# Attention and expert FFN on one core: first loads reordered, router product narrowed, last chunk finished in halves

## The reference, cut

```python
x = x + xattn(_layernorm(x), ctx, ctx, mask, Wq, Wk, Wv, Wo, W1, b1, W2, b2, gamma, beta)   # 8 heads of 128
x = x + ffn(_layernorm(x), router_w, bias, gate_w, up_w, down_w, sh_gate_w, sh_up_w, sh_down_w)

# xattn: q, k, v per head; A = softmax(mask(q @ k.T)); proj = (A @ v) @ Wo
x = _layernorm(value + proj, gamma[0], beta[0])
x = _layernorm(x + relu(x @ W1 + b1) @ W2 + b2, gamma[1], beta[1])

# ffn: 16 experts in 4 groups, 2 groups and 4 experts kept per token, 2 shared experts for all
topk_idx, tw = _route(x, router_w, bias)
y = einsum('etf,efd->etd', silu(h) * u, down_w)           # h, u: gate and up products of each expert
routed = einsum('etd,te->td', y, combine)
sh = silu(x @ sh_gate_w) * (x @ sh_up_w) @ sh_down_w
```

## Time and profile before

| | |
|---|---|
| time, median of 3 runs | 303.92 us (303.61 to 304.14) |
| the profiled execution: its own time | 303.7 us |
| its span, first to last instruction | 301.9 us |
| TensorE busy | 288.1 us, 95% |
| VectorE, GpSimd, ScalarE busy | 189.1, 183.4, 157.6 us |
| mean granted TensorE clock | 0.999 |

### The profile page before, as it was taken

The page is one execution under the profiler, slowest core; times in us unless marked ns, Lnnn a source line. Parts: engine busy times, 40 slices in busy tenths (PEclk is TensorE's granted clock), DMA queues, the critical chain, the costliest instruction groups (busy, mean ns, idle before and its releaser), DMA issues.

```text
span 301.9 us, 4524 instructions
## 1 busy us (share of the span) xinstructions
PE 288.1 (95%) x1446; PEld 209.1 (69%) x1446; DVE 189.1 (63%) x490; ACT 157.6 (52%) x292; POOL 183.4 (61%) x165
## 2 busy tenths in 40 slices
PE   2799999999999999999999999999999999999974
PEld 2566667857774788787677766776678888678853
DVE  0456787558758785764568544366956665866673
ACT  1457727768586468643435253372256455545551
POOL 2336678555377684105878856566507778988870
PEclk9999999999999999999999999999999999999999
DMA  6993600030001100007431342310055345343001
GB/s 220 261 281 67 253 0 3 0 106 1 2 0 34 73 0 1 2 0 275 154 113 53 116 134 85 127 72 0 2 150 210 139 108 182 126 141 112 29 2 69
DMA packets 8711, 27.97 MB, mean 93 GB/s; under 512 B 1136, under 2 KB 1904, under 8 KB 8560
## 3 DMA queue, kind: packets, MB, share of 16 engines
q1 hardware_dynamic: 8400, 26.63, 27.3%
q10 hardware_dynamic: 288, 1.05, 0.9%
HBM read 26.49 MB, written 1.18 MB: 92 GB/s over the span
## 4 chain that ended last, share of the span: by engine, by line
PE 95%; DVE 2%; DMA 2%; ACT 1%; issue 0%; DVEq 0%
PE bank L1394 17%; PE bank L1396 16%; PE bank L1395 16%; PE bank L1605 10%; PE bank L1480 10%; PE bank L1468 6%; PE bank L1440 5%; PE bank L1449 3%; PE bank L1511 2%; PE bank L1504 2%; PE bank L1545 2%; DMA w_in<-in_w_attn 2%; DVE act_lo L1191 1%; PE bank L1533 1%; PE bank L1611 1%; PE bank L1413 1%
## 5 line engine op out<-in xcount | busy, mean ns | idle before, releaser
L474 POOL TENSOR_TENSOR k_T<-xnT,k_T 128x512 f32<-128x512 f32 x64 | 94.3, 1479 | 40.4 <-DVE xnT L1186 25.1
L747 ACT ACTIVATE xnT<-bank 128x512 f32<-128x512 f32 x72 | 43.0, 599 | 76.3 <-PE bank L1396 76.2
L1186 DVE TENSOR_TENSOR xnT<-bank,xnT 128x512 f32<-128x512 f32 x64 | 43.9, 690 | 54.4 <-PE bank L1396 26.9
L1394 PE MATMUL bank<-mT_hi,we_hi 128*128 128x512 f32 x144 | 60.4, 420 | 0.0
L1396 PE MATMUL bank<-mT_hi,we_lo 128*128 128x512 f32 x144 | 56.8, 395 | 0.0
L1395 PE MATMUL bank<-mT_lo,we_hi 128*128 128x512 f32 x144 | 56.8, 394 | 0.0
L1480 PEld LDWEIGHTS bank<-vo,o_T 128*128 128x128 f32 x256 | 30.0, 192 | 5.5 <-issue 3.8
L1605 PE MATMUL bank<-k_T,w_in 128*128 128x512 f32 x72 | 33.0, 592 | 0.0
L1394 PEld LDWEIGHTS bank<-mT_hi,we_hi 128*128 128x128 f32 x144 | 27.1, 188 | 8.2 <-issue 2.3
L1395 PEld LDWEIGHTS bank<-mT_lo,we_hi 128*128 128x128 f32 x144 | 27.1, 188 | 7.2 <-issue 1.7
L1480 PE MATMUL bank<-vo,o_T 128*128 128x128 f32 x256 | 32.1, 279 | 0.0
(11 more groups left out here) (126 smaller groups left out, 492.0 us busy)
## 6 DMA issues: line engine op xcount, KB each, us to landing
k_T<-comb_dram SPq DMA_DIRECT2D x32, 512.0 KB, 3.7
w_in<-in_w_gu SPq DMA_DIRECT2D x3, 768.0 KB, 4.2
w_in<-in_w_dn SPq DMA_DIRECT2D x1, 1152.0 KB, 7.2
w_in<-in_w_attn ACTq DMA_DIRECT2D x2, 512.0 KB, 5.4
w_in<-in_w_attn SPq DMA_DIRECT2D x2, 512.0 KB, 10.7
out_x<-ctx_all SPq DMA_DIRECT2D x4, 256.0 KB, 3.3
ctx_swap<-in_ctx_in SPq DMA_DIRECT2D x2, 384.0 KB, 14.3
ctx_all<-in_ctx_in SPq DMA_DIRECT2D x2, 256.0 KB, 6.4
```

Source lines behind the costliest of these rows:

```text
L474: pool.tensor_tensor(act[n % 4], s_u[n % 2], comb[u % RING][:, c % 2 * CW:(c % 2 + 1) * CW], ALU.mult).then_inc(weighed_ready, 1)
L747: a.activation(silu[n % 2], h_bank[n % 2][:], ACT.Silu).then_inc(silu_ready, 1)
L1186: v.tensor_tensor(into, u_bank[n % 2][:], silu[n % 2], ALU.mult).then_inc(s_u_ready, 1)
L1394: pe.matmul(dst, w_hi, m_hi, start=start, stop=False)
```

## The change

- **Loads.** ScalarE's queue now carries the first chunk of the context, the first chunk of x, and Wq and Wk in four quarters of two heads. SyncE's queue begins with the mask column and then waits until the second quarter has landed before it issues anything else.
- **Start on TensorE.** `turn_ctx(0)` comes first, then folds of two heads each; the first two keys stand behind three of the four quarters. Both folds of Wv and Wo stand ahead of `scores(0)`.
- **Router.** `route` multiplies with the 16 router columns alone.
- **Last chunk.** Steps 69, 70 and 71 are f32 products again. Chunk 3 is copied out, turned (into two free banks), added and stored in two halves. `act_low` stands two steps back.
- **Order.** Most of the lists between the start and step 41 are written in a new order. Normalisation 2 of chunks 2 and 3 is on ScalarE. `gate(0)` and `gate(1)` stand ahead of `router_sigmoid(0)`, and `dn_low` 1 to 3 stand some 20 steps earlier.

```diff
-        ld_w = [[sem(f"ld_w{i}{half}") for half in range(2)] for i in range(2)]
+        ld_w = [[sem(f"ld_w0{q}") for q in range(HP)], [sem(f"ld_w1{half}") for half in range(2)]]
-        fold_bank = [bank[6], bank[5], bank[2], bank[3]]
+        fold_bank = [bank[6], bank[5], bank[2], bank[3], bank[2], bank[3]]
+        SPLIT_TO = N - 3
+        def split(n):
+            return SPLIT_FROM <= n < SPLIT_TO
         def split_count(n):
+        last_bank = [h_bank[0], u_bank[0]]
...
-            context(0, 1, ld_c0)
             sp.dma_start(mask_col[:], mask_tok).then_inc(ld_mask_col, 16)
-            rows(0, 1, ld_x0)
+            sp.wait_ge(ld_w[0][1], 16)
             context(1, 2, ld_c1)
...
-            sp.wait_ge(fold_done, 4)
+            sp.wait_ge(fold_done, 6)
...
-            def store(c):
-                sp.wait_ge(out_ready, c + 1)
-                sp.dma_start(out[:, c * TPC:(c + 1) * TPC, :], x2[:, c * TPC:(c + 1) * TPC, :]).then_inc(stored, 16)
+            def store(c, half=None):
+                first, count = (0, TPC) if half is None else (half * 2, 2)
+                tiles = slice(c * TPC + first, c * TPC + first + count)
+                sp.wait_ge(out_ready, c + 1 + (half or 0))
+                sp.dma_start(out[:, tiles, :], x2[:, tiles, :]).then_inc(stored, 16)
...
-            store(3)
-            sp.wait_ge(stored, 16 * CH)
+            for half in range(2):
+                store(CH - 1, half)
+            sp.wait_ge(stored, 16 * (CH + 1))
```

On ScalarE and VectorE:

```diff
-            for half in range(2):
-                a.dma_start(w_in[:, 0, half], w_attn[:, 0, half]).then_inc(ld_w[0][half], 16)
+            def quarter(q):
+                pair = slice(q % 2 * 2, q % 2 * 2 + 2)
+                a.dma_start(w_in[:, 0, q // 2, pair], w_attn[:, 0, q // 2, pair]).then_inc(ld_w[0][q], 16)
+            a.dma_start(ctx_all[:, 0:TPC, :], ctx_in[:, 0:TPC, :]).then_inc(ld_c0, 16)
+            a.dma_start(x_all[:, 0:TPC, :], x[:, 0:TPC, :]).then_inc(ld_x0, 16)
+            for q in range(HP):
+                quarter(q)
...
-            def copy_out(c):
+            def copy_out(c, cols=slice(0, CW)):
...
-                a.copy(acc_out[c], acc[c][:]).then_inc(acc_copied[c], 1)
+                a.copy(acc_out[c][:, cols], acc[c][:, cols]).then_inc(acc_copied[c], 1)
...
-                if n - 3 >= SPLIT_FROM:
-                    act_low(n - 3)
+                if n >= 2 and split(n - 2):
+                    act_low(n - 2)
...
-            for n in range(N - 3, N):
-                act_low(n)
             add_out(2)
-            add_out(3)
+            add_out(3, 0)
+            add_out(3, 1)
```

On TensorE, with the new `fold` and `turn_out`:

```diff
-                    last = pe.matmul(xm_bank[c][:, t * P:(t + 1) * P], xm_T[:, t * P:(t + 1) * P], small_T[:],
+                    last = pe.matmul(xm_bank[c][:, t * P:t * P + NE], xm_T[:, t * P:(t + 1) * P], small_T[:, 0:NE],
                                      start=True, stop=True)
...
+            def fold(i, part):
+                pe.wait_ge(ld_w[i][part], 16)
+                if i == 0:
+                    half, heads, a, b = part // 2, range(part % 2 * 2, part % 2 * 2 + 2), 1, 0
+                    into = fold_bank[part]
+                else:
+                    pe.wait_ge(fold_lo, HP - 1 + part)
+                    half, heads, a, b = part, range(HP), 0, 1
+                    into = fold_bank[HP + part]
+                for k, h in enumerate(heads):
+                    last = pe.matmul(into[:, k * P:(k + 1) * P], w_in[:, i, half, h, a, :], w_in[:, i, half, h, b, :],
+                                     start=True, stop=True)
                 last.then_inc(fold_done, 1)
...
-                if n >= SPLIT_FROM:
+                if split(n):
...
+            def turn_out(c, half=None):
+                into = acc[c] if half is None else last_bank[half]
+                first, count = (0, TPC) if half is None else (half * 2, 2)
+                pe.wait_ge(acc_copied[c], 1 if half is None else half + 1)
+                for t in range(first, first + count):
+                    last = pe.transpose(into[:, t * P:(t + 1) * P], acc_out[c][:, t * P:(t + 1) * P], ident[:])
                 last.then_inc(out_turned, 1)
```

More of the change, by code:

```diff
@@ L973, in _ @@
             gate(33)
-            for n in range(34, N):
+            gate(34)
+            gate(35)
+            gate(36)
+            gate(37)
+            act_high(36)
+            copy_out(0)
+            act_high(37)
+            copy_out(1)
+            gate(38)
+            gate(39)
+            act_high(38)
+            gate(40)
+            act_high(39)
+            gate(41)
+            for n in range(42, N):
                 gate(n)
-                if n - 2 >= SPLIT_FROM:
+                if n >= 2 and split(n - 2):
                     act_high(n - 2)
@@ L1640, in _ @@
             key(1, 5)
-            fold(1, 1)
+            turn_probs(0)
             key(1, 6)
-            turn_probs(0)
+            key(1, 7)
+            attend(0)
+            scores(3)
             turn_xn(1)
-            key(1, 7)
-            scores(3)
-            attend(0)
+            turn_ctx(2)
+            project(0)
             turn_probs(1)
-            turn_ctx(2)
             scores(4)
-            project(0)
-            scores(5)
             key(2, 0)
@@ L1673, in _ @@
+            key(2, 6)
+            attend(3)
             turn_probs(4)
+            project(2)
+            turn_probs(5)
+            attend(4)
+            key(2, 7)
             project(3)
-            attend(4)
-            turn_probs(5)
-            key(2, 5)
-            key(2, 6)
+            scores(8)
+            turn_probs(6)
+            attend(5)
+            turn_ctx(3)
             turn_xn(3)
-            key(2, 7)
-            turn_ctx(3)
-            attend(5)
-            scores(8)
@@ L1685, in _ @@
-            key(3, 1)
-            key(3, 0)
-            turn_x1(0)
-            project(4)
-            ffn_up(0, 0)
-            scores(9)
-            turn_probs(6)
+            scores(9)
+            project(4)
+            scores(10)
+            turn_x1(0)
+            turn_probs(7)
+            key(3, 0)
+            scores(11)
+            ffn_up(0, 0)
+            key(3, 2)
+            key(3, 1)
             ffn_up(0, 1)
-            scores(10)
-            turn_probs(7)
+            attend(6)
@@ L1713, in _ @@
-            key(3, 6)
+            attend(9)
+            project(8)
+            turn_probs(10)
             turn_xm(0)
-            project(8)
-            scores(12)
-            turn_probs(10)
+            scores(13)
+            attend(10)
+            turn_probs(11)
             route(0)
-            scores(13)
+            scores(14)
+            project(9)
             turn_x1(1)
-            attend(9)
+            scores(15)
             ffn_up(1, 0)
-            scores(14)
+            project(10)
@@ L1778, in _ @@
             up(12)
+            down(6)
+            down(7)
+            down(8)
+            down(9)
+            turn_xm(2)
             up(13)
[L1780 to L1782 removed]
+            up(14)
             down(10)
[L1784 to L1786 removed]
             down(11)
             down(12)
[L1789 removed]
+            up(15)
             up(16)
             up(17)
+            down(13)
+            down(14)
             up(18)
             up(19)
[L1794 to L1795 removed]
+            up(20)
+            route(2)
             down(15)
```

633 lines of the change are left out of this document (316 added, 317 removed).

## The result

The changed kernel takes **300.24 us** (median of 4 executions, 299.78 to 300.31), the kernel before 303.85 beside it (303.61 to 304.14). The measured ratio is 0.9863, with a 95% interval of 0.9834 to 0.9892; the two medians printed here make 0.988, which lies inside it. So the kernel is 1.2 to 1.4% faster, clearly more than the 0.2% that could be told. The forecast was 299.2 in a range of 296.8 to 301.4. The time lies in the range and 1.0 us above the forecast. The profiled span fell from 301.9 to 298.5 us, 3.4 us, where the terms of the sum made 4.5.

What follows compares the result with a forecast made beforehand. TensorE, busy 95% of the span, was taken as the bound, with gains left at the two ends. 303.7 - 2.7 (start) + 0 (router) + 0.4 (middle) - 2.2 (end) = 299.2 us, range 296.8 to 301.4.

Steps and rivals of the forecast that it cites:

- Start: From launch to the transposes behind the eighth key: 15.6 instead of 18.32, -2.7 us, bounds -1.0 and -3.7.
- the landing: First context load, alone on its queue: estimated 2.5 us from issue, landing at 3.3; upper bound 4.3, landing at 5.1.
- start gives back: Rival at the start: clock or context late, more keys at half pace, only 1.0 us gained, 300.9 us; chance 0.16.
- Its 0.5 us: At the start: if the clock counts from the first fold, 1.0 us later, the rise costs 0.5 us, giving 299.7.
- Router: Routing products, four times 8 instructions: 16 columns instead of 128 save 0, as weight loads are not narrowed; other bound 3.1.
- The rival of 3.1 us: Routing products: moving columns set the pace, 3.1 us less, 296.1 us; half of it, 297.6; chance 0.13.
- Middle: New order between the two ends: waits added and removed sum to +0.4 us, bounds -0.9 and +2.
- `turn_xm(1)` to `route(1)`: Neighbouring steps on TensorE in the middle: copy, last transpose's way and hand-over between them cost +0.8 us.
- `project(14)` to `project(15)`: Neighbouring projections in the middle sharing one bank: `add_ctx` and hand-over between them cost +0.5 us.
- the one on the routing: VectorE's way from logits to weights, 13.95 us, taken as just hidden behind 14.3 us of TensorE work; bound 1 us.
- End: From `down(67)`'s last matmul to the span's end: f32 last steps and halves, 299.7 instead of 301.9, -2.2 us.
- Slower than before: Rival from step 42 on: each `act_low` starts inside a weighing, +0.35 us in 30 steps, 309.7 us; chance 0.05.

Runs made afterwards that it cites:

- the warmed-up kernel: The changed kernel with eighteen 128x128 f32 transposes of the identity matrix ahead of `turn_ctx(0)`: 299.19 us, ratio 0.9836.
- the one with the pairs apart: The changed kernel with `project(14)` between `turn_xm(1)` and `route(1)`, and `route(1)` between the last two projections: 299.34 us, ratio 0.9836.
- two more kernels: The changed kernel with pairs apart, `dn_low(1)` moved and transpose warm-up together, 297.58 us; the same with SyncE waiting for the first weight quarter, 297.73 us.

## Why the prediction was right, and where it was off

- **Start, -2.7 forecast, -2.12 in the trace of after.** The step that failed is the landing, and the clock made up for a part. The context was put at 2.5 us from issue to landing, alone on its queue, an estimate from no row; it took 3.6, with x and the quarters issued behind it from 1.22 on, and `mask_context` began at 4.48. That the quarters would be there when their folds came up, at 5.4, 6.3 and 7.2, is shown by no row or run: they landed at 6.54, 7.22 and 7.87. The first was read at 6.58, 0.25 behind the start of the last transpose. They were just in time because the context was late too; in the warmed-up kernel the folds do wait for them, a little. The first key came at 9.16 instead of 8.15. But by then the clock had all but risen (9.5, as forecast), so that only one key matmul ran slow instead of 1.4 us of them. That 9.5 is luck: the forecast had the rise 5 us behind a first transpose at 4.4, and it came 3.9 us behind one at 5.66. The rise is not at a fixed time: with the same instructions the twelve folds took 2.93 us in after, 2.77 in the kernel with `dn_low(1)` moved and 2.53 in the one with the pairs apart, and the transposes behind the eighth key stood at 16.20, 15.97 and 15.62. The start is thus worth 2.1 to 2.7 us, the upper end being the forecast by another way. How much of it is the quarters and how much the transposes' place, no run separates.
- **The rival "start gives back"** named the right weakness, clock and landing, but the reason given for it fell: transposes raise the clock. Its 0.5 us is what was measured, by way of the landing.
- **Router, 0 forecast.** The eight take 0.91 us in after, 0.89 in the earlier trace rows. The rival of 3.1 us is excluded. For its half, the interval of the kernel with the router alone would leave 0.2 to 1.6 us; its median is 0.2 lower, and the trace, with the same stride and a span 0.1 longer, leaves nothing.
- **Middle, +0.4 forecast, +0.93 in the trace.** `turn_xm(1)` to `route(1)` was put at +0.8 (spacing +0.89, wait 0.68), `project(14)` to `project(15)` at +0.5 (+0.72, wait 0.47), `ffn_down(1)` at -0.3 (-0.28). The sum missed the wait at 202 us (+0.95). The step that failed is the one on the routing: the way from the logits to the weights was counted for chunks 0 and 1, found just hidden, and the second half's was not looked at. There the new order had put `dn_low` between two weighings, the very pattern whose going the same paragraph had booked as a gain. More was saved elsewhere than forecast, 1.63 instead of 0.9, and by luck the error stayed at 0.5.
- **End, -2.2 forecast, -2.2 in the trace.** The last addition ends at 296.07, two halves of 0.75 together from 295.32 on, where 295.0 was forecast for a kernel 1 us quicker. The working gave the gain to the last steps in f32 alone; the runs show that it is half that and half `act_low(n - 2)`, without which `down(68)` waits 0.84.
- **Slower than before** by `act_low` inside the weighings did not come: in after its 33 instructions take 0.69 us in the mean, and none is waited for:

```profile
L1229 DVE TENSOR_TENSOR act_lo<-k_T,act_hi 128x512 fp32r<-128x512 f32 x33 | 22.8, 690 | 1.6 <-ACT act_hi L776 1.6
```

- **What the prediction did not see at all** is how little the parts are worth alone. It priced the held-back loads at nothing, as a mere order of issue; without that one wait the kernel is 1.5% slower than before. And it took the order for a cost of 0.4, whereas without the order the start brings nothing that can be told, and without `act_low(n - 2)` the end brings half.

## What to carry to other kernels

An earlier start pays only as far as the order behind it asks for things at the new times: after moving the start, read the waits of the next 30 us, not only of the first. Loads issued early on a second queue take bandwidth from the ones that are waited for; where the urgent ones are issued late, as here, a wait on the issuing engine until they have landed was worth 9 us. And where VectorE works on two SBUF tiles at once beside a row of GpSimd instructions, look for instructions of one kind whose duration differs by a factor of four.

## What the runs showed of the hardware that was not expected

- Transposes by TensorE alone bring its clock up. In three executions of the same start the slow pace ended between 8.6 and 9.5 us, with the engine at work since 5.6; with the transposes as a warm-up, at work since 1.41, it ended at 6.2 us, and in two more kernels before 5.7. With waits of 4.0, 2.7 and 1.0 us in between it lasted until 19.5.
- The first 256 KB load of a queue took 3.6 us at the start of the program, 3.2 with SyncE's loads issued as well; the four quarters of 256 KB behind it took 5.1 (median) with SyncE held back and 12.9 with everything issued.
- VectorE's instructions on two SBUF tiles wait for the end of GpSimd's running one, and of several in a row: 0.28 us became 0.98 to 1.37, each ending 0.15 us behind GpSimd's. GpSimd's weighings wait for VectorE's in the same way, 1.34 to 1.82 us instead of 1.26 to 1.30.
- 128x16 routing matmuls in f32 follow each other at the 0.11 us of 128x128 ones; each loads 128 columns of weights, and a load lasts 192 ns.
